# Layer 0's middle reordered: shared products in banks of their own and around the counts, the token list ahead of the shared multiplications, half of the shared down products behind the expert loop

## The reference, cut to what matters

```
x = x + layernorm(ffn0(layernorm(x)))

def ffn0(x):
    logits = x @ router_w.T + router_b
    top_vals, top_idx = top_k(logits, 4)
    rw = softmax(top_vals) * 1.8
    combine = einsum('tke,tk->te', one_hot(top_idx, 32), rw)
    g = silu(einsum('th,eih->tei', x, gate_w))          # i = 192
    u = einsum('th,eih->tei', x, up_w)
    routed = einsum('tei,ehi,te->th', g * u, down_w, combine)
    shared = silu(x @ shared_gate_w.T) * (x @ shared_up_w.T) @ shared_down_w.T
    return routed + shared
```

## Time and profile before

| | |
|---|---|
| median of three runs | 931.89 us |
| the profiled execution, device time | 925.98 us |
| its span (first to last instruction) | 924.1 us |
| TensorE busy | 714.6 us, 77% |
| VectorE busy | 497.7 us, 54% |
| ScalarE busy | 343.5 us, 37% |
| GpSimd busy | 281.8 us, 30% |
| layer 0's second half, router to the first transposition of the loop | 218.4 to 258.9 us |
| layer 0's expert loop | 258.9 to 491.4 us |

### The profile page before, as it was taken

One profiled execution on the slowest core, in us unless ns is written; L12 is line 12 of the kernel. 1 busy time (PEld: TensorE's weight loads), 2 busy tenths in 40 slices (PEclk: granted clock), 3 DMA queues, 4 the chain that ended last, 5 costly groups with the idle time before them and its releaser, 6 DMA issues. The chain is left out here.

```text
span 924.1 us, 14171 instructions
## 1 busy us (share of the span) xinstructions
PE 714.6 (77%) x4395; PEld 465.5 (50%) x4395; DVE 497.7 (54%) x1370; ACT 343.5 (37%) x726; POOL 281.8 (30%) x311
## 2 busy tenths in 40 slices
PE   4879999966787787778881387899995599878890
PEld 2433443245476676667770252334423446767780
DVE  3489776056723333433445688877904862334447
ACT  3345657722322222222220444357683241322211
POOL 2040111210065565555451037011122003455530
PEclk9999999975899989997996597999999699999896
DMA  2533011401336666666656034202002100566654
GB/s 82 160 123 101 2 30 42 142 1 46 104 117 199 205 215 211 196 211 209 201 163 222 0 116 129 88 1 97 2 1 96 53 2 25 174 191 213 213 184 162
DMA packets 64200, 109.27 MB, mean 118 GB/s; under 512 B 14922, under 2 KB 40932, under 8 KB 64020
## 3 DMA queue, kind: packets, MB, share of 16 engines
q1 hardware_dynamic: 54868, 94.52, 32.2%
q0 software_dynamic: 9216, 14.06, 4.7%
q10 hardware_dynamic: 64, 0.03, 0.0%
HBM read 85.15 MB, written 19.99 MB: 114 GB/s over the span
## 5 line engine op out<-in xcount | busy, mean ns | idle before, releaser
L1284 DVE TENSOR_REDUCE mx<-ps 128x1 f32<-128x512 f32 (+3 forms) x304 | 180.3, 656 | 52.0 <-PE ps L715 36.9
L1051 ACT ACTIVATE X<-ps 128x1024 f32<-128x1024 f32 (+1 forms) x192 | 146.1, 810 | 80.1 <-PE ps L741 79.5
L914 PE MATMUL ps<-X,KA 128*128 128x128 f32 x1152 | 158.7, 292 | 9.7 <-ACT X L1138 6.0
L914 PEld LDWEIGHTS ps<-X,KA 128*128 128x128 f32 x1152 | 149.3, 207 | 13.7 <-issue 11.9
L621 POOL DMA_INDIRECT KA<-token_rows,row_of_slot x96 | 98.6, 1027 | 142.9 <-DVE row_of_slot L1458 107.4
L628 POOL DMA_INDIRECT outs<-X,token x96 | 97.3, 1014 | 129.7 <-DVE mine L1508 50.6
L1522 DVE TENSOR_TENSOR X<-ps,X 128x128 f32<-128x128 f32 x96 | 27.9, 291 | 183.0 <-ACT X L1148 138.0
L712 PE MATMUL ps<-KA,QA 112*128 112x512 bf16 (+3 forms) x384 | 113.6, 344 | 9.8 <-DVE mx L1284 4.9
L925 PE MATMUL ps<-KA,X 128*128 128x256 f32 x192 | 66.1, 429 | 55.7 <-DVE X L1525 44.4
L602 POOL TENSOR_SCALAR_AFFINE_SELECT X<-X 128x512 f32<-128x512 f32 x64 | 40.7, 637 | 206.1 <-ACT X L1051 206.1
L741 PE MATMUL ps<-QA,KA 114*128 114x512 bf16 (+3 forms) x384 | 93.3, 329 | 6.3 <-ACT X L1051 6.0
(11 more groups left out here) (216 smaller groups left out, 911.0 us busy)
## 6 DMA issues: line engine op xcount, KB each, us to landing
KA<-in_ex SPq DMA_DIRECT2D x96, 512.0 KB
KA<-in_dn SPq DMA_DIRECT2D x96, 64.0 KB
outs<-empty SPq DMA_DIRECT2D x4, 1024.0 KB, 7.6
X<-outs SPq DMA_DIRECT2D x8, 512.0 KB, 6.1
V<-outs SPq DMA_DIRECT2D x8, 512.0 KB, 7.4
QA<-X SPq DMA_DIRECT2D x28, 128.0 KB, 2.5
KA<-X SPq DMA_DIRECT2D x28, 128.0 KB, 2.5
QA<-w_sdn SPq DMA_DIRECT2D x28, 128.0 KB, 2.4
```

The lines of the kernel that those rows point to most:

```text
L914: mm = pe.matmul(ps[:, 2 + r % 2, m * P:(m + 1) * P], w_ex[:, w, col:col + P], rowsT[:, r % 2, k, :], start=(k == 0), stop=(k == KD - 1))
L1051: nc.scalar.activation(probs[:, st % PB, 2 * p:2 * p + 2, off:CH], ps[:, 4 + 2 * p:6 + 2 * p, off:CH], ACT.Exp, scale=SCALE).then_inc(S(f" ...
L1284: v.tensor_reduce(mx[:, part, i, h0:h0 + nh], ps[:, n % RB, 0:nh * w].rearrange("p (h w) -> p h w", h=nh), AX.X, ALU.max)\
```

## The change

Four edits, all in layer 0's second half; layer 1 has the same order and banks as before.

1. **Banks.** The four units of shared products get banks of their own: unit 0 in 0 and 1, unit 1 in 2, unit 2 in 3 and 6, unit 3 in 7. Units 2 and 3 no longer wait for `s_act`. The shared down products use banks 0 and 1.
2. **Around the counts.** Only the gate half of unit 0 stands ahead of the counts. The up half follows `begins`, and units 1, 2 and 3 all follow the product for `texp_ps`.
3. **The list first.** On VectorE all four quarters of the list come right behind `in_tile`, then `shared_mult(0)` and `(1)`, then `tokens`, then `shared_mult(2)` and `(3)`.
4. **Half of the down products behind the loop.** `shared_down` of tiles 0 to 3 stands ahead of the expert loop, that of tiles 4 to 7 behind it, on TensorE and on ScalarE. The loop's first transposition waits for four copies in place of eight, and VectorE waits for all eight ahead of the second chunk's sum.

```diff
+def shared_bank(L, i):
+    return (6 if L == 1 and i < TPC else 0) + i % 2
+
+def up_bank(L, u, x):
+    return (0, 2, 3, 7)[u] + x * (1, 0, 3, 0)[u] if L == 0 else 2 * (u % 2) + x
...
-                def shared_up(u):
+                def shared_up(u, those=(0, 1)):
                     n, j = divmod(u, nsc)
-                    if u >= 2:
+                    if L == 1 and u >= 2:
                         pe.wait_ge(S(f"s_act{L}"), u - 1)
-                    for x in range(2 if j < SFULL[L] else 1):
+                    those = those if j < SFULL[L] else those[:1]
+                    for x in those:
...
-                    mm.then_inc(S("s_gu"), 1)
-
-                shared_up(0)
-                if L == 1:
+                    if those[-1] == 1 or j == SFULL[L]:
+                        mm.then_inc(S("s_gu"), 1)
+
+                if L == 0:
+                    shared_up(0, (0,))
+                else:
+                    shared_up(0)
                     shared_up(1)
...
                       .then_inc(S("begins"), 1)
-                    shared_up(1)
+                    shared_up(0, (1,))
...
                       .then_inc(S("texp_ps"), 1)
+                    shared_up(1)
...
-                for i in range(NT if L == 0 else TPC):
+                for i in range(TPC):
                     shared_down(i)
...
-                pe.wait_ge(S("sh_sb"), NT + TPC * L)
+                pe.wait_ge(S("sh_sb"), NT * L + TPC)
...
-                for i in range(TPC if L == 1 else NT, NT):
+                for i in range(TPC, NT):
                     shared_down(i)
...
-                    shared_mult(0)
-                    shared_mult(1)
                     dve.wait_ge(S("in_tile"), 1)
                     for q in range(QUARTERS):
                         token_lo(q)
                         at_places(q)
-                        if q == 1:
-                            shared_mult(2)
+                    shared_mult(0)
+                    shared_mult(1)
+                    tokens()
+                    shared_mult(2)
                     shared_mult(3)
-                    tokens()
...
+                    if L == 0 and n == 1:
+                        dve.wait_ge(S("sh_sb"), NT)
```

25 lines of the change are left out of this document (15 added, 10 removed).

## The result

The changed kernel takes 923.84 us (median of 19 runs) against 931.78 for the kernel before (19 runs beside them). The ratio is 0.9906, with a 95% interval of 0.9884 to 0.9928: 8.8 us less, 6.7 to 10.8.

A forecast was written before the change was run, and what follows sets the result against it. The prediction took the expert loop's start, set by the list of slots and its gathers, as the bound. An earlier `in_tile` (1.5 us) and a shorter way to `tokens` made 5.4 us: 931.89 - 5.4 = 926.5 us, range 923.2 to 932.0.

The forecast's parts named there:

- The bound: Start of the expert loop: it follows the list (`row_of_slot`) and the burst of gathers, whatever TensorE did before.
- Part 1: Half of unit 0 ahead of the counts: counts 2.3 us earlier, of which 1.5 us are left for `in_tile`.
- Part 2: List first, from `in_tile` to `tokens`: 7 us in place of 11, so `tokens` starts 5.4 us earlier in all.
- Part 3: Ahead of the loop: gathered rows last with 1.4 us to spare; gain between 5.4 and 7.5 us, taken as 5.4.
- The mechanism that I gave for following the gathers: Loop's second silu on ScalarE: handed over only when the burst of nine gathers is through, 1.20 us after the last.
- Part 4: Four down products behind the loop: hidden by ten microseconds of loads and sums, cost nothing; 3.6 + 0.5 us without cover.
- The clock that stays low: Rival: TensorE's low clock goes on until 241, so the gain is 3.9 us, 928.0 us; chance 0.10.
- TensorE's first transposition as the pace: Rival: the loop follows TensorE, not the gathers, and gains 7.5 us, 924.4 us; chance 0.14.
- The loop that swallows the shift: Rival: two more stalls before down products in the loop take 5.4 us, 931.9 us, the same within 0.3%; chance 0.20.
- The slower case: Rival: four more stalls in the loop, 10.8 us, give 937.3 us; chance 0.10.

The follow-up runs named there:

- e13: Changed kernel with 36 idle repeats of VectorE's first copy of `tokens` ahead of it, so the list comes late: 847.5 us, 1.0074 of the kernel before.
- e2: Kernel before with only the move of four shared down products behind the loop: 841.9 us, 1.0010 of the kernel before.
- e14: Changed kernel with 18 more matmuls on TensorE between the four shared down products and the loop's first transposition: 840.6 us, 0.9995 of the kernel before.
- e9: Changed kernel again, nothing edited, on the third chip: 923.5 us, 0.9945 of the kernel before.
- e5: Kernel before again, nothing edited, on the second chip: 935.3 us, 1.0020 of the kernel before.
- e6: Changed kernel again, nothing edited, on the second chip: 928.1 us, 0.9919 of the kernel before.
- e15: Changed kernel again, nothing edited, on the fourth chip: 835.2 us, 0.9934 of the kernel before.

## Why the prediction came out as it did

**The bound** was read rightly in the main: the list, then the gathered rows. e13 shows it directly, and e2 shows the converse, a TensorE that is early for nothing (0.8 us more +-1.9). "Whatever TensorE did before" was too strong: e14 has the list in time and loses 5.4 us to a late TensorE.

**Part 1 is the step that failed.** The counts came where I put them: `cnt` moved by 2.43 us where I had 2.3. But I wrote "the rank matmuls ... from 229.6 and doubled", and so left 1.5 us of the 2.3; that term of the sum is mis-sized. In the changed kernel the clock was indeed at 0.50 until 231.7, through nearly all the ranks, and they took 1.09 us from the end of the counts (230.72 to 231.81), against 1.0 at the full clock. Those small bf16 matmuls hardly stretch, though float32 rows do, the router's of 32 columns (3.98 to 6.88 us) as well as the wide ones. From `tbeg` on VectorE's own chain sets the pace: `texp_i` was 5.60 us behind the picks in after and 5.58 in e9, whether the up half of unit 0 took 1.98 or 3.66 us. The term was 1.5 and measured 2.43. Of the 3.4 us by which the measurement (8.8) exceeds the sum (5.4) this explains 0.9. The other 2.5 us are seen at no place in the profiles. The three later measurements gave 7.6, 5.1 and 5.6, so they may be scatter of the first, but their cause stays open. The clock also rose 1.4 us behind the picks, where before it was 1.7; I had 6 to 10. The Trainium skill, "TensorE: Matmul & The Clock Gate", Part 4, says of transposes that they don't count as busy in the same way. I had stretched that to narrow matmuls, and the stretch was not borne out for the ranks between two wide products: the low clock did not go on.

**Part 2 was right to a tenth.** From the end of `in_tile` to `tokens` it is 7.08 us (forecast 7.05); of 11.03 us, 3.95 are gone. TensorE's products were done 10.8 us behind the picks (241.1) and not 14.4 (243.5 in the forecast), since the clock had come up, and cost nothing either way. Part 1 and 2 together are 6.4 and not 5.4. That holds for the course of the clock that the profile before showed. Where the router had the full clock (e5 and e9) part 1 gains nothing and part 2 gains 4.96, from 12.03 to 7.07 us; the list is then 5.0 us earlier.

**Part 3 was wrong in its detail, and that was harmless here.** I had the copies done by 249.9, 20.8 us behind the picks, and the rows last with 1.4 us to spare. The list had left gaps in TensorE's work, the clock fell, and the four down products took 6.59 us in place of 3.6, the copies until 253.3, 23.0 behind the picks. The rows were then 2 us early. With a fast router (e9) the products take 3.69 us and the rows are last, as forecast.

The mechanism that I gave for following the gathers, a hand-over that comes only when the burst is through, is not borne out. The second silu comes 1.2 to 1.4 us behind the burst's last gather in before, e5, after and e6; but in e9 the last gather starts at 254.61 and ends at 255.61, and the silu is at 255.29; on the fourth chip, in e15, it comes three gathers before the end. Nor does the silu keep its distance from `row_of_slot` once TensorE's part is changed: 13.7 us in before and after, 12.2 in e9, 8.5 in e15 and 14.6 in e14. I chose the 5.4 over the 7.5 of the first transposition by this mechanism, and the choice rests on nothing that held. The change moved both chains by nearly the same, 6.4 and 6.6 us, and that is luck.

**Part 4 was right**, ten microseconds of cover and no wait. I missed that the four products that stay can keep the clock up, as in e15, though they did not in e9.

**The rivals.** The clock that stays low did not come. TensorE's first transposition as the pace, 7.5 us, lies nearer to the first measurement (8.8) than my sum, and would have been taken for right by it. Four measurements give 7.0 +-1.3, which 6.4 and 7.5 fit and 5.4 does not, so the size alone doesn't refute it. e2 speaks against it: its transposition was 2.2 us earlier than e5's, and it gained nothing. e13 and e14 don't separate the two, since the first transposition moved with the delay in both (by 9.2 and 6.8 us). The loop that swallows the shift: its length does scatter by +-5 us on the chips with waits, but around the same mean, 221 and 232 in before, 225 to 228 in after. Its premise, that the stalls are set by how gathers, scatters and weight loads fall together, is shown by no run; what sets them stays open. The slower case has no run.

## What to carry to other kernels

Work moved to the other clock should not be scaled by it where no row shows the like of it there; keep both prices and see whether it is on the path at all. Find the instruction from which the later stage has a constant length (here the second silu, 163.6 us from the end of the loop on the chips without waits) and count a gain by how far that moves, with a delay put on one chain at a time to tell which of two it follows. One profile can stand for a course of the clock, or of the loop, that most executions don't take: look at several before pricing an edit of 2 us. An order that puts one consumer off is only as good as the buffers that let its producer go on; undo the two apart before crediting either.

## What the runs showed of the hardware

**The same program takes 841 or 932 us, by the chip.** Layer 0's loop, from the first transposition to the last down product, of the changed kernel and then of e15, the same program:

```profile
253.57:486.67 233.10, 177.12 (x1153) 158.35 (x1154) 86.09 (x325) 57.16 (x192) 124.48 (x123) 0.94 0.59 191
```

```profile
249.29:418.65 169.36, 162.81 (x1153) 147.91 (x1154) 87.65 (x326) 59.42 (x192) 126.15 (x124) 0.99 0.83 263
```

Single instructions are as long on either: 1.50 us for twelve up rows, 1.00 for a gather. But the same 1153 matmuls take 233.1 us in one and 169.4 in the other. Of the 63.7 us between them, 47.0 are TensorE's wait before a down product (47.4 us over the whole loop in after, 0.4 in e15), and 14.3 are matmuls that took longer, at a mean granted clock of 0.94 against 0.99. In those waits an up product's row has ended and ScalarE takes it up some 4 us later, VectorE right behind it, as at 257.6 to 261.5 above; GpSimd went on with its gathers through that one. What holds them isn't shown by these traces and stays open. A 0.3% effect must be measured against runs on the same chip.

**The clock takes one of two courses through the router**, in either kernel: its 32 rows take about 4 (3.76 to 4.26) or 6.88 us, and the second picks are ready at 224.5 to 227.1 or at 228.0 to 230.3. The Trainium skill, "TensorE: Matmul & The Clock Gate", "What's actually happening", calls the warm-up run-variable, and the trace agrees (216.20 3.98 in e9, 0.50 throughout in the earlier trace rows). By its place in the profiles edit 2 is worth 2.4 us in one course and nothing in the other, so a single profile says little of its worth.
